# Message rows of a graph network's first edge stage added into two DRAM tables in turn instead of four

## The reference

```python
h = x @ W_in
Wij = ssp(f_ij[:, 0, :] @ W_f1 + b_f1) @ W_f2 + b_f2
x_ij = h[idx_j] * Wij * f_ij_cutoff
agg = jax.ops.segment_sum(x_ij, idx_i, num_segments=n_atoms)
out = ssp(agg @ W_o1 + b_o1) @ W_o2 + b_o2
```

## Time and profile before

| what | us |
|---|---|
| median of 2 runs | 5342.42 (5338.36 to 5346.49) |
| profiled execution, device time | 5346.22 |
| its span, first to last instruction | 5344.4 |
| mean granted TensorE clock in the span | 0.843 |
| first scatter (L859) starts | 140.4 |
| last scatter starts | 1715.7 |

### The profile page before, as it was taken

One profiled execution on the slowest core, in us unless ns is written; L12 is line 12 of the kernel. 1 busy time (PEld: TensorE's weight loads), 2 busy tenths in 40 slices (PEclk: granted clock), 3 DMA queues, 4 the chain that ended last, 5 costly groups with the idle time before them and its releaser, 6 DMA issues.

```text
span 5344.4 us, 89296 instructions
## 1 busy us (share of the span) xinstructions
PE 4027.9 (75%) x26176; PEld 3581.8 (67%) x26176; DVE 3142.9 (59%) x11560; ACT 1649.0 (31%) x3533; POOL 3676.1 (69%) x3340
## 2 busy tenths in 40 slices
PE   3776767667774477778778777777799888698887
PEld 2655555555553477777777756676688787588886
DVE  3655555555552567777777756666566565355555
ACT  3444444444442333333333333323211111011010
POOL 0788888888887076666666556767677777667776
PEclk9877777777776777777778889999899999799998
DMA  7666666666665322222222222222344444444443
GB/s 211 128 116 116 116 111 113 116 116 114 112 115 69 98 56 52 49 52 52 50 50 52 43 67 53 54 52 55 102 136 141 139 131 149 142 158 159 149 150 110
DMA packets 412959, 541.56 MB, mean 101 GB/s; under 512 B 139471, under 2 KB 324408, under 8 KB 405944
## 3 DMA queue, kind: packets, MB, share of 16 engines
q0 software_dynamic: 199680, 221.72, 24.2%
q1 hardware_dynamic: 178524, 289.13, 17.3%
q10 hardware_dynamic: 34396, 26.36, 1.7%
HBM read 383.80 MB, written 153.13 MB: 100 GB/s over the span
## 4 chain that ended last, share of the span: by engine, by line
PE 38%; DMA 17%; issue 15%; POOL 13%; DVE 12%; DVEq 2%; ACT 1%; SPq 1%; POOLq 0%; ACTq 0%
DMA sums<-G,idx 15%; POOL sums L859 9%; PE psC L1386 8%; PE psF L1386 7%; PE psC L1318 5%; POOL G L835 4%; PE psA L1308 4%; PE psE L1369 4%; PE psD L1369 3%; PE psA L1355 2%; PE psB L1355 2%; DVE S L2129 2%; DVE mc_mx L1793 1%; DVE early L2117 1%; PE psD L1323 1%
## 5 line engine op out<-in xcount | busy, mean ns | idle before, releaser
L835 POOL DMA_INDIRECT G<-table,idx x1664 | 1602.4, 963 | 682.6 <-issue 588.0
L859 POOL DMA_INDIRECT sums<-G,idx x832 | 1283.7, 1543 | 340.7 <-issue 161.5
L816 POOL DMA_INDIRECT G<-table,idx x832 | 786.9, 946 | 410.6 <-issue 272.3
L1090 ACT COPY arena<-psA 128x600 f32<-128x600 f32 x312 | 205.7, 659 | 1157.3 <-PE psA L1355 1145.7
L1258 PE MATMUL psE<-arena,stage 128*128 128x128 f32 x832 | 211.3, 434 | 454.9 <-ACT G L1019 454.8
L1258 PEld LDWEIGHTS psE<-arena,stage 128*128 128x128 f32 x832 | 181.2, 321 | 539.6 <-ACT G L1019 539.6
L1386 PE MATMUL psC<-arena,stage 128*128 128x144 f32 (+1 forms) x3822 | 501.5, 290 | 22.7 <-DMA arena<-adjacency 14.4
L1710 DVE TENSOR_TENSOR arena<-psB,G 128x1024 f32<-128x1024 f32 x104 | 127.3, 1224 | 654.8 <-PE psB L1239 654.7
L1386 PEld LDWEIGHTS psC<-arena,stage 128*128 128x128 f32 x3822 | 488.7, 199 | 25.0 <-issue 24.1
L1386 PE MATMUL psF<-arena,stage 128*128 128x144 f32 (+1 forms) x3822 | 499.4, 289 | 0.0
L1386 PEld LDWEIGHTS psF<-arena,stage 128*128 128x128 f32 x3822 | 487.2, 198 | 0.0
(11 more groups left out here) (296 smaller groups left out, 8194.6 us busy)
## 6 DMA issues: line engine op xcount, KB each, us to landing
adjacency<-arena SPq DMA_DIRECT2D x26, 2400.0 KB
arena<-adjacency SPq DMA_DIRECT2D x26, 2400.0 KB
acc<-in_src_row SPq DMA_DIRECT2D x104, 512.0 KB
arena<-in_dst_row SPq DMA_DIRECT2D x104, 512.0 KB
G<-table,idx POOLq DMA_INDIRECT x2496
sums<-G,idx POOLq DMA_INDIRECT x832
sums<-arena ACTq DMA_DIRECT2D x4, 3300.0 KB, 39.6
table<-cut ACTq DMA_DIRECT2D x147, 64.0 KB
```

Of the source, the lines that this page charges most:

```text
L816: pool.indirect_dma_start(G[st.r][:, t * width:(t + 1) * width], None, tables[n], bass.IndirectOffsetOnAxis(ap=idx[st.r][:, t:t + 1], axis ...
L835: pool.indirect_dma_start(G[at.r][:, t * D:(t + 1) * D], None, tables[n], bass.IndirectOffsetOnAxis(ap=idx[at.r][:, t:t + 1], axis=0)).the ...
L859: pool.indirect_dma_start(sums_dram[t % SUMS], bass.IndirectOffsetOnAxis(ap=idx[st.r][:, t:t + 1], axis=0), G[st.r][:, t * TW:(t + 1) * TW ...
L1090: A.copy(dense_at(at.g, m.loaded + j, at.place), counts_in((c * m.built + j) % 2)).then_inc(mixed["kept"], 1)
```

## The change

`SUMS`, the number of tables, is 2 instead of 4. All that is written over `range(SUMS)` or modulo `SUMS` follows from it: two tables are cleared and read back, tile t of a chunk goes to table t % 2 and waits for the scatter of tile t-2 (of tiles 6 and 7 of the chunk before for t = 0 and 1), and PE accumulates two matmuls where it had four.

```diff
 TILES = 8
 CHUNK = P * TILES
 ROWS = 4
-SUMS = 4
+SUMS = 2
 NODES_PER_BATCH = 7
 EPS = 1e-5
```

## The result

| | before | after |
|---|---|---|
| median, us | 5342.42 | 5750.49 (5745.74 to 5755.24, 2 runs) |
| ratio | | 1.0765, 95% interval 1.0739 to 1.0791 |
| span of the profiled execution, us | 5344.4 | 5743.9 |
| first to last scatter | 140.4 to 1715.7 | 129.2 to 2133.6 |
| layer 0 loop, first to last scatter | 1575.3 | 2004.4 |

The kernel is 7.6% slower. The span grew by 399.5 us: +429.1 in the loop, -11.2 ahead of it, -28.8 in the read-back, and +10.4 in layers 1 to 3, whose program is the same.

The account below looks back on a forecast made before the run. POOL's own pace of scatters was taken to bound the layer 0 loop. The span, 5344.4 + 482 (loop) - 24 (read-back) - 13 (clears) = 5789 us, plus 1.8 around it gave 5791 us, range 5705 to 5905.

Parts of the forecast that it names:

- Pairs: Layer 0 loop: two scatters, one on each table, take 4.05 us instead of 3.7; four pairs make 16.2 us a chunk.
- The load window: Layer 0 loop: while SP loads a chunk, scatters land late, adding 3.6 us once a chunk (2.8 to 4.1).
- The loop term: Layer 0, first to last scatter: 103.9 chunks of 19.8 us, 2057 us instead of 1575.3, +482 us.
- Who waits: Layer 0 loop: ACT's wait at L1004 grows by 4.6 us a chunk from 6.5; no engine takes POOL's place.
- The read-back: Adding the tables after the loop: PE's batch falls from 10.2 to 6.7 us, -24 us (-15 to -28).
- The clears: Kernel start: with half the clears, the last load lands at 43 instead of 56 us, -13 us (0 to -20).
- The cross-check by stepping the scatters: Layer 0 loop: 832 scatters stepped through the wait rules with the trace's landings gave 2000 to 2120 us.
- the tiles' own landings: Rival, layer 0 loop: each tile's landing lasts as long as before, three held a chunk, 5903 us; chance 0.14 with worse.
- The hidden window: Rival, layer 0 loop: SP's loads fall where a table waits anyway, 5417 us; chance 0.05, hidden in part included.
- Shorter landings with less in flight: Rival, layer 0 loop: landings fall under 2.95 us, POOL keeps its 1.85 us pace, 5309 us; chance 0.03.

## Why the prediction was right

The direction and the mechanism held, and the time lay in the range: 5791 was said, 5750 measured, an increase of 408 where 449 was forecast. By the steps:

- *Pairs.* Said: 3.3 + 0.75 = 4.05 us instead of 3.7. Measured: 4.05, and 4.09 a scatter with one table. The run with a wait two places back on four tables shows that nothing else of the change is in it.
- *The load window.* This is the term that was mis-sized. I took 3.6 us a chunk, between 2.8 and 4.1; it is 19.3 - 16.2 = 3.1. The loop term came out +429 where +482 was said. The reason given, "because both are held in a window and the later landing decides", does not fit its rows: in the earlier trace rows the later landing is that of the scatter begun at 619.09, whose excess is the 2.8, and the 4.1 is the excess of the earlier one. Taken over 91 windows of each trace, it is the longest landing that decides: in 84 of the 91 windows of the changed kernel it is a link of the chain. On average it is 6.4 us there, 3.1 over the undisturbed one. Before the change it was 6.8, 3.5 over, close to the 3.6 taken. So what failed in the term is that it kept the landings of the old pace, and at the new pace they are shorter. That goes with the pace and not with the number of tables: it is 6.5 us with four tables and a wait two places back. Why it is so was not tried. That the long landings come from SP's loads is shown by the runs with shorter ones.
- *Who waits.* ACT's wait was to grow to 11 us a chunk and is 10.7; the idle time before L859 was to be 820 us and is 770, short by the same 50 us. It was to be put down to the DMA, and the profile does so for 389 us only; the rest is POOL's own 0.30 us at each scatter and releases, as said above. The last scatter was to start near 2185 and starts at 2133.6, for the same reason.
- *The read-back.* A batch takes 6.6 us (6.7 said). The term is -28.8 instead of -24: the first loads came in sooner too, and PE began 5.2 us after them (2136.9 to 2142.1) instead of 8.4 (1719.2 to 1727.6), where I had allowed 1 us.
- *The clears.* The last load landed at 44.7 (43 said), the first scatter came 11.2 us earlier (13 said).
- *The rest.* Layers 1 to 3 took 10.4 us more, which no term had. In the eleven other traces of this study, with this same code, it takes 3489 to 3517 us, so one execution tells nothing of 10 us.

The sum of terms against the measured: 482 - 24 - 13 = 445 said; 429 - 29 - 11 + 10 = 399 measured. Two small slips stand in the recorded numbers: with 2.8 us for the window the sum gives 5708 and not 5705, and 28.7 + 39.6 is 68 and not 67. The cross-check by stepping the scatters had 2000 to 2120 us for the loop; 2004.4 lies at its lower end, so it held better than the single price.

Of the rivals, the tiles' own landings (5903) is out: a slower pace does put fewer scatters into a window, 2.1 with landings over 3.7 us on average where there were 3.3 before. The hidden window (5417) is out: even 208 KB of loads still have a price. Shorter landings with less in flight is out for the undisturbed ones: with one table and nothing else in flight the landing is 3.3 us. In the windows there is something to it: the longest is 6.8, 6.4 and 5.9 us on average with four, two and one table, which is where the 3.6 came out too high. It may also come from where in a window a scatter falls; no run tells the two apart.

With 3.3 us measured, the Trainium skill's estimate ("DMA: Bandwidth & Descriptors", section "Anatomy of one DMA - SWDGE (gpsimd) path"), 2.2 us for this transfer, cannot stand for the time that a chain on one table sees. Counted from the end of POOL's instruction (3.27 - 1.54 = 1.7 us) the landing is nearer to it, but the instruction and the 0.75 us of release are in the chain as well, 4.05 us in all.

## What to carry to other kernels

When DMAs that must not overlap are spread over n buffers, one landing plus the release must fit into n issue times. Work out n from the longest landing that other traffic causes, not from the undisturbed one. Here 7.4 + 0.75 = 8.15 us over 1.85 is 4.4: four tables leave the longest uncovered, which cost 39 us, and a fifth was not tried. Spreading the other traffic helps as well: with the loads split, four tables cover it. Fewer buffers save clearing and merging (40 us here), which is paid once, while the wait is paid in every step. Before giving up buffers for their clearing, look at when the clearing runs: behind the loads that all wait for, four tables started 16 us earlier than two did with the clears beside the loads.

## What was not expected of the hardware

Two loads of 512 KB close together or some 7 us apart cost the chain of scatters the same (2004.4 and 2002.9 us), since every long landing is in its sum. With the four-table wait only the first form shows at all (39 us), since there only the longest single landing counts (6.8 against 5.2 us on average). And loads cut to a fifth of their bytes still cost 0.9 of 3.1 us a chunk, more than their share.
